# Second layer of a two-layer attention and expert kernel: the last block of weights is loaded, cast and subtracted at an earlier place

## The reference, cut to what matters

```python
xn = _layernorm(x)
x = x + _L0_attn_ref(xn, ...) + _L0_ffn_ref(xn, ...)   # linear attention, 32 heads; 16 experts, 2 chosen per token, and a shared one
xn = _layernorm(x)
x = x + _L1_attn_ref(xn, Wqkv, bqkv, Wo, bo) + _L1_ffn_ref(xn, A, B, Wr)
```

```python
scores = xf @ Wr.T
top_vals, top_idx = jax.lax.top_k(scores, 16)
G = zeros(N, 64).at[rows, top_idx].set(softmax(top_vals))
h = jnp.einsum('nd,krd->nkr', xf, A)
out = jnp.einsum('nkr,kdr->nd', h * G[:, :, None], B) * 2.0
```

## Time and profile before

| | |
|---|---|
| median of 3 runs | 2505.82 us (2503.87 to 2508.46) |
| profiled execution, its own time | 2502.5 us |
| span of the profiled execution, first to last instruction | 2500.7 us |
| PE busy | 2439.5 us (98%) |
| DVE, ACT, POOL busy | 1575.7, 1348.0, 1591.5 us |
| TensorE clock granted over the span | 0.994 of full speed |

### The profile page before, as it was taken

The page is one execution under the profiler, slowest core; times in us unless marked ns, Lnnn a source line. Parts: engine busy times, 40 slices in busy tenths (PEclk is TensorE's granted clock), DMA queues, the critical chain, the costliest instruction groups (busy, mean ns, idle before and its releaser), DMA issues.

```text
span 2500.7 us, 42232 instructions
## 1 busy us (share of the span) xinstructions
PE 2439.5 (98%) x13818; PEld 2118.4 (85%) x13818; DVE 1575.7 (63%) x2437; ACT 1348.0 (54%) x2668; POOL 1591.5 (64%) x1529
## 2 busy tenths in 40 slices
PE   8999999999999999999999999999999999959999
PEld 6888888898989898788888888888889878847887
DVE  6565565757574747886565565657575779865554
ACT  5556555556565555555555565555565558732221
POOL 5666767676676764767676767777776678732210
PEclk9999999999999999999999999999999999989999
DMA  4210211111111112211121111111111179931110
GB/s 160 87 56 31 63 49 44 55 46 55 38 55 46 51 44 91 99 55 56 31 63 47 46 55 44 53 42 55 39 58 43 32 263 305 305 122 34 51 34 34
DMA packets 89454, 183.36 MB, mean 73 GB/s; under 512 B 12626, under 2 KB 38882, under 8 KB 89366
## 3 DMA queue, kind: packets, MB, share of 16 engines
q1 hardware_dynamic: 80822, 165.41, 20.4%
q0 software_dynamic: 8544, 16.82, 2.3%
HBM read 163.28 MB, written 26.79 MB: 76 GB/s over the span
## 4 chain that ended last, share of the span: by engine, by line
PE 87%; DVE 4%; DMA 3%; issue 2%; POOL 2%; ACT 1%; SPq 0%; POOLq 0%; DVEq 0%; ACTq 0%
PE bank L102 27%; PE bank L103 27%; PE bank L104 27%; DMA exin<-xn_rows,ecur 2%; PE bank L1144 2%; PE bank L1117 2%; DVE acc L2892 1%; POOL el L2527 1%; POOL exin L2498 0%; PE bank L2378 0%; SPq L3035 0%; POOL acc L2183 0%; PE bank L574 0%; DVE xl L585 0%; PE bank L2775 0%
## 5 line engine op out<-in xcount | busy, mean ns | idle before, releaser
L2039 POOL TENSOR_TENSOR wl<-w_in,wh 128x512 fp32r<-128x512 f32 x510 | 621.8, 1246 | 304.5 <-ACT wh L1443 301.5
L102 PE MATMUL bank<-xh,wh 128*128 128x512 f32 x1400 | 556.9, 398 | 0.7 <-DVE bank L1750 0.5
L104 PE MATMUL bank<-xh,wl 128*128 128x512 f32 x1400 | 545.6, 390 | 0.0
L103 PE MATMUL bank<-xl_sums,wh 128*128 128x512 f32 x800 | 312.3, 390 | 0.0
L104 PEld LDWEIGHTS bank<-xh,wl 128*128 128x128 f32 x1400 | 262.9, 188 | 56.7
L102 PEld LDWEIGHTS bank<-xh,wh 128*128 128x128 f32 x1400 | 263.5, 188 | 52.9 <-DVE bank L1750 4.4
L2057 POOL TENSOR_TENSOR sqacc<-sqacc,sq 128x512 f32<-128x512 f32 x128 | 173.3, 1354 | 198.6 <-ACT sq L1428 194.0
L1443 ACT CAST wh<-w_in 128x512 fp32r<-128x512 f32 x502 | 261.9, 567 | 32.2 <-POOL w_in L533 32.2
L102 PE MATMUL bank<-wh,xh 128*128 128x256 f32 x912 | 259.3, 284 | 0.1
L103 PE MATMUL bank<-wl,xh 128*128 128x256 f32 x912 | 258.6, 284 | 0.0
L1787 DVE TENSOR_TENSOR acc<-bank,acc 128x512 f32<-128x512 f32 x240 | 162.3, 686 | 118.2 <-PE bank L104 115.9
(11 more groups left out here) (380 smaller groups left out, 6368.3 us busy)
## 6 DMA issues: line engine op xcount, KB each, us to landing
w_in<-in_w_pairs_dram SPq DMA_DIRECT2D x100, 512.0 KB, 3.8
o_in<-in_o_pairs_dram SPq DMA_DIRECT2D x32, 512.0 KB, 3.5
eraw<-in_ex_dram SPq DMA_DIRECT2D x31, 513.0 KB, 5.8
y_slots<-ey SPq DMA_DIRECT2D x30, 512.0 KB, 4.3
w_in<-in_w_pairs_dram SPq DMA_DIRECT2D x56, 256.0 KB, 3.0
dcur<-in_decay_dram SPq DMA_DIRECT2D x32, 256.0 KB, 3.0
eraw<-in_ex_dram SPq DMA_DIRECT2D x31, 256.0 KB, 3.9
out_dram<-acc SPq DMA_DIRECT2D x16, 256.0 KB, 2.0
```

What stands on the lines that cost most here:

```text
L102: pe.matmul(out, wh, mh, start=start and i == 0, stop=False, skip_group_check=True)
L103: pe.matmul(out, wh, ml, start=False, stop=False, skip_group_check=True)
L104: ins = pe.matmul(out, wl, mh, start=False, stop=stop and i == n - 1, skip_group_check=True)
L2039: pool.tensor_tensor(wl[:, cols], w_in[:, cols], wh[:, cols].bitcast(F32), ALU.subtract).then_inc(w_lo, 1)
```

## The change

The constant EARLY is 8, which is NR. SP no longer waits for the gathers: the 16 DMAs follow the load of `l_bq` directly (the wait stays in the text under `k == EARLY`, which no k reaches). ACT casts all eight ranks ahead of its first event, `stats` (0,0), with one wait for all 16 DMAs. POOL subtracts all eight ranks behind the eight gathers of group 0, then issues `gather(1, 0)`, adds `l_bo` to group 0's tiles, and issues `gather(1, 1)` behind these additions, no longer ahead of them.

```diff
-LATE_COLS = D
+LATE_COLS, EARLY = D, 8
...
-    late_high = {("score", 0, 0): (0, 1, 2), ("scores_t", 0, 0): (3, 4, 5), ("score", 0, 1): (6, 7)}
...
     def scalar(a):
+        def late_high(k):
+            cols, src = late_cols[k]
+            if k in (0, EARLY):
+                a.wait_ge(dma_late, 16 * ((PIECES + 1) // 2 + 2 * (NR if k else EARLY)))
+            a.copy(w1h[:, cols], w1_late[:, src]).then_inc(a_late, 1)
+
+        for k in range(EARLY):
+            late_high(k)
         for what, g, i in events:
-            for k in late_high.get((what, g, i), ()):
-                cols, src = late_cols[k]
-                if k == 0:
-                    a.wait_ge(dma_late, 16 * ((PIECES + 1) // 2 + 2 * NR))
-                a.copy(w1h[:, cols], w1_late[:, src]).then_inc(a_late, 1)
...
-        late_low(0, 1, 2, 3)
+        late_low(*range(EARLY))
         gather(1, 0)
         pool.wait_ge(dma_bo, 16)
         for g in range(NG):
-            if g == 0:
-                late_low(4, 5, 6, 7)
-                gather(1, 1)
             for t in range(g * TPG, (g + 1) * TPG):
                 if t % TPG == 0:
                     pool.wait_ge(q["v_xn"], g + 2)
                 pool.tensor_tensor(acc[:, t, :], acc[:, t, :], bo[:], ALU.add).then_inc(q["p_bo"], 1)
             if 0 < g < NG - 1:
                 gather(g + 1, 0)
+            if g < NG - 1:
                 gather(g + 1, 1)
 
     def sync(sp):
         sp.dma_start(bq[:], b_qkv).then_inc(dma_c, 16)
 
-        sp.wait_ge(dma_y[1][TPG - 1], 16)
         for k in range(NR):
+            if k == EARLY:
+                sp.wait_ge(dma_y[1][TPG - 1], 16)
             for j in range(2):
                 to = w1_late[j:P:2, k * D:(k + 1) * D]
                 sp.dma_start(to, by_gate[NR * j + k]).then_inc(dma_late, 16)
```

## The result

The changed kernel took 2512.66 us (median of 8 runs, 2508.25 to 2517.79) against 2505.76 for the kernel before beside it: ratio 1.0025, 95% interval 1.0013 to 1.0037. A second set of 11 runs gave 2508.74 against 2506.36, ratio 1.0014 (1.0004 to 1.0023). It is slower, by about the 0.2% (5 us) that the prediction took for the limit of what can be told from no change.

What follows compares the result with a forecast made beforehand. PE, busy 2439.5 of 2500.7 us, was taken to bound the kernel. First `xt` 13.2 us later against 13.8 given back made -0.6, 2501.9 profiled; with the median 3.3 above, 2505.2, range 2500.8 to 2510.6.

Steps and rivals of the forecast that it cites:

- the delay of the first `xt`: Front of group 0: first `xt` 13.2 us later, 11.0 from the later root and 2.2 from POOL's subtractions beside DVE.
- The weights' landing: Late weights, issued at 2199.30 and sharing the DMA engines with group 0's gathers at 0.92, land at 2216.0.
- The upper bound, 20.9: Latest landing, 2220.2, if the late weights run at half their speed while the gathers are in flight.
- ACT: Ahead of the first root: eight casts take 4.3 us, then the 1.28 us table load; root 11.0 us later.
- POOL against DVE: POOL's eight subtractions beside DVE's first scaling pair: 1.8 us for the pair plus 0.4 for tile 2's additions.
- my upper bound: DVE's first scaling pair held until POOL's run of subtractions ends, costing 3.4 us.
- Back: From group 0's attention to group 1's `xt`: ACT free, shorter second `l_p` pair and earlier `l_bo` additions return 13.8 us.
- Sum: Whole kernel: +13.2 - 13.8 = -0.6 us, profiled execution 2501.9, median stated as 2505.2.
- Rival (b): Front: weights land at 2220.2 (+4.2) and DVE is held to POOL's run's end (+1.2); +4.8, 2510.6; chance 0.11.
- My sign of being wrong: First cast later than 2220, or PE still waiting for `l_p` or at the second `outputs`.
- rival (a): Front: weights lose nothing to the gathers (-1.8), DVE slips between subtractions (-2.2); -4.6, 2501.2; chance 0.13.
- Rival (c): Long DVE instructions have another cause, so only 1.9 us return; 11.3 us slower, 2517.1; chance 0.04.

Runs made afterwards that it cites:

- additions moved: Kernel before with one POOL wait added, so group 0's four bias additions wait for group 1's normalised rows; ratio 0.9981 to the kernel before.
- subtract late: Changed kernel with POOL's eight subtractions moved behind the additions of group 0's bias; ratio 1.0060 to the kernel before.
- two waits: Changed kernel with ranks 0 to 3 and 4 to 7 on semaphores of their own instead of one wait; ratio 1.0015 to the kernel before.
- combined version: Changed kernel with split weight waits, casts behind both roots, subtractions behind group 0's last `xt`, bias additions later; two versions, ratios 0.9950 and 0.9944 to the kernel before.

## Why the prediction was wrong

I gave 2505.2 us, range 2500.8 to 2510.6, and the kernel took 2512.66. The structure of the sum held: two large terms that nearly cancel. One of them, the delay of the first `xt`, was 4.4 us too small.

- **The weights' landing** failed most. I had 16.7 us from first issue to landing (2216.0 - 2199.3); it was 20.0: +3.3. The failed step is dividing the engine time by 0.92, the share of the experts' stretch. The amount was nearly right, the rate was not. The two stretches are shown below.
  13.5 x 0.80 + 4.0 x 0.44 = 12.6 us of all 16 engines against my 13.6. But the two streams together ran at 0.80, not at the experts' 0.92, and at the end, with the gathers done, the rest of the weights ran at 0.44, close to the 0.47 that they reached by themselves before (the gathers by themselves reached 0.63). Why the two together stay at 0.80 no run here shows. The upper bound, 20.9, held. That streams issued from SP and from GpSimd interleave on the same 16 engines is what the Trainium skill says ("DMA: Bandwidth & Descriptors", section "Issuing engines are not separate DMA queues"). The 20.0 against 14.4 us agrees.
- **ACT** was right: eight casts 4.26 us (4.3), the table load 1.28 behind them, root 5.57 us behind the landing (5.6).
- **POOL against DVE**: 3.4 us beyond the 2.4 of an idle POOL, where I took 2.2. I counted the scaling pair and missed the three tiny steps ahead of it, each of which waits out one subtraction (0.81, 1.18, 1.19). One subtraction each was the right rule for an instruction that arrives inside a run; applied to these it fills the run to its end, my upper bound. This is the second term that was mis-sized: 3.4 instead of 2.2. First `xt` 17.6 us later instead of 13.2.
- **Back**: 13.3 instead of 13.8. The parts: to attention's output 8.7 instead of 9.0, of which 0.4 is the copy of the router's scores, held up behind the first `l_p` pair (6.13 us, foreseen, its cover priced at 0.1); then 4.6 instead of 4.8 to `xt` of group 1, checked alone with "additions moved" (5.1, from the first `xt` on: 63.8 us before, 58.8 there).
- **Sum**: +17.6 - 13.3 = +4.3 instead of -0.6. Rival (b), the weights crawling behind the gathers and DVE held to the run's end, is what happened, priced at +4.8 and measured at +4.3, its landing 0.9 us short of the price; I had given it 0.11. Landing 3.3 us late lay inside my own bounds and the held DVE at their edge, so 0.72 for "within 5 us" and a point below zero leant on two middle values at once, both on the kind side. The median came out 2 us above the range's end, which I had put exactly at that rival's price with no room for scatter. With the measured +4.3 my own sum gives 2502.5 + 3.3 + 4.3 = 2510.1; the 2.6 us up to 2512.66 are no more than the scatter between sets of runs: the second set, of the same kernel, has its median at 2508.74, 3.9 us lower and within the range. My sign of being wrong, a first cast later than 2220, was set too late: on the clock of the kernel before the cast came at 2219.3 (2197.75 + 21.55), and the first `xt` at 2230.6 instead of 2226.2. (The range's lower end, 2500.8, is also 0.4 below the 2501.2 of rival (a).)
- **Rival (c)**, that the long DVE instructions have a cause other than POOL, is out: "additions moved" took the additions away and the 7.80 went to 2.74; "subtract late" lengthened POOL's run behind the gathers and the first `l_p` pair went from 6.13 to 15.86.

The two stretches of the first point, in the view by stretches of the changed kernel (the last columns are the granted clock, the DMA share and the GB/s):

```profile
2203.00:2216.50 13.50, 0.00 (x0) 0.00 (x0) 4.81 (x9) 0.00 (x0) 6.96 (x8) 0.53 0.80 258
2216.50:2220.50 4.00, 0.00 (x0) 0.00 (x0) 0.00 (x0) 0.00 (x0) 0.00 (x0) 0.50 0.44 170
```

## What to carry to other kernels

A step that waits for a whole load costs the landing, not its own time, once it is put ahead of the only instruction another engine waits for: ask what is queued behind it in that stream, and put the step behind that instruction, in the engine's next idle time. Split such a wait before moving it (two waits gave 3.1 of 4.3 us back in the profiled execution). A run of POOL work beside DVE should be charged to every DVE instruction of the kinds that were held here, however small: TENSOR_TENSOR with both inputs in SBUF, TENSOR_SCALAR and SCALAR_TENSOR_TENSOR (a RECIPROCAL was not held). Additions that nothing needs for 50 us (done from 2257.55 on in the kernel before, first read at 2315.13) should stand where DVE is not on the path: that one move was worth 5 us, and the combined version 14.

## What the hardware showed that I had not expected

- A DVE instruction that starts while POOL is issuing a gather, straight ahead of back-to-back POOL instructions, waits for all of them: 5.6 to 5.9 us for four, 15.60 us for twelve (0.35 us alone). One that arrives inside such a run waits for about one of them, or for what is left of it (0.8 to 1.2 us where 0.16 was due). The first case was seen in ten of the twelve profiled executions (not in the combined versions, where no POOL run stands straight behind a gather), the second in eleven (not in "subtract late"). Gathers without a run behind them hold nothing: `combine` in the changed kernel started at 2266.36, beside the gathers of 2265.40 and 2266.65, and took 2.73 us. Why the two cases differ was not tried.
- The Trainium skill, "SBUF — State Buffer", section "Who interferes with whom", has it of DVE in its two-port modes that whoever issues first has the shared pair for the whole instruction and the other blocks. In "subtract late" DVE started at 2247.29 and POOL's first addition at 2247.96, and DVE finished 15.6 us later; POOL's twelve took 1.22 to 1.25 us each. The gather that was under way may count as POOL's claim, which no run here shows; in any case the loser did not wait for one instruction but for the run.
- The same code ahead of E brought E to between 2197.75 and 2207.12 in twelve profiled executions. A difference of 4 us between two spans says nothing without a common mark.
